# Turning softmax probabilities by 32x32 blocks and transfers, not by TensorE

## What is computed

```
# layer 0                              # layer 1 (8 heads of 64)
h = x @ W                              q, k, v = h @ Wq.T + bq, h @ Wk.T + bk, h @ Wv.T + bv
e = leaky_relu(h@a0 + (h@a1).T)        scores = q @ k.T / 8, -inf where adj == 0
alpha = softmax(e, -1e9 where adj==0)  attn = softmax(scores)
out = concat([alpha @ h, h])           out = (attn @ v) @ Wo.T + bo
x1 = layernorm(x + out)                y = layernorm(x1 + out)
```

## Time and profile before

| | us |
|---|---|
| median of 3 runs (lowest to highest) | 3468.7 (3466.77 to 3469.16) |
| the profiled execution, its whole time | 3468.5 |
| its span in the trace | 3466.6 |
| busy: TensorE, VectorE, ScalarE, GpSimd | 3412.3, 2688.1, 2510.2, 1616.8 |
| one steady round | 106.0 |

### The profile page before, as it was taken

The page is one execution under the profiler, slowest core; times in us unless marked ns, Lnnn a source line. Parts: engine busy times, 40 slices in busy tenths (PEclk is TensorE's granted clock), DMA queues, the critical chain, the costliest instruction groups (busy, mean ns, idle before and its releaser), DMA issues.

```text
span 3466.6 us, 65791 instructions
## 1 busy us (share of the span) xinstructions
PE 3412.3 (98%) x23168; PEld 2903.8 (84%) x23168; DVE 2688.1 (78%) x7607; ACT 2510.2 (72%) x5382; POOL 1616.8 (47%) x1542
## 2 busy tenths in 40 slices
PE   6999999999999999999999999999999999999998
PEld 5888888888888888888888888888888888888886
DVE  5787777877777877778777778777787777877776
ACT  4776777776777767777777777677777777777775
POOL 2544454445454444544454544445444454444443
PEclk8999999999999999999999999999999999999999
DMA  3000011000111010110001110001100011100100
GB/s 128 19 22 28 25 38 38 31 26 22 34 38 38 20 31 25 37 38 31 26 21 36 38 35 22 26 31 38 38 25 32 19 38 37 32 25 25 31 13 25
DMA packets 59652, 111.19 MB, mean 32 GB/s; under 512 B 6720, under 2 KB 7488, under 8 KB 59328
## 3 DMA queue, kind: packets, MB, share of 16 engines
q1 hardware_dynamic: 59328, 106.99, 9.6%
HBM read 73.41 MB, written 33.55 MB: 31 GB/s over the span
## 4 chain that ended last, share of the span: by engine, by line
PE 97%; DVE 1%; ACT 1%; issue 0%; DMA 0%; POOL 0%; SPq 0%; ACTq 0%; DVEq 0%; POOLq 0%
PE R_bank L541 47%; PE O_bank L629 14%; PE T_bank L613 14%; PE S_bank L603 13%; PE L_bank L541 5%; PE L_bank L532 3%; PE L_bank L556 0%; DMA prob<-WkT 0%; POOL turned L985 0%; DVE prob L900 0%; PE O_bank L541 0%; DMA alpha<-a 0%; ACT tokens L674 0%; DVE n_wide L946 0%; ACT prob L734 0%
## 5 line engine op out<-in xcount | busy, mean ns | idle before, releaser
L965 POOL TENSOR_TENSOR prob<-prob,rsum 128x512 f32<-128x512 f32 x1024 | 1059.5, 1041 | 1309.3 <-DVE rsum L906 1307.4
L734 ACT ACTIVATE prob<-prob,negmax 128x512 f32<-128x512 f32 x1024 | 739.6, 722 | 323.3 <-DVE negmax L900 314.9
L659 ACT ACTIVATE probT<-T_bank 128x512 fp32r<-128x512 f32 x1024 | 579.0, 594 | 220.8 <-PE T_bank L613 214.6
L900 DVE CUSTOM_DVE_ANT_0 prob<-S_bank,mask 128x512 f32<-128x512 f32 x1024 | 695.5, 679 | 2.2 <-PE S_bank L603 1.1
L794 DVE TENSOR_TENSOR probT<-T_bank,probT 128x512 fp32r<-128x512 f32 x1024 | 675.9, 683 | 5.1 <-ACT probT L659 3.1
L613 PE MATMUL T_bank<-ident,prob 128*128 128x128 f32 x4096 | 597.7, 276 | 3.1 <-DVE probT L794 3.1
L629 PE MATMUL O_bank<-probT,v_st 128*128 128x256 f32 x4096 | 586.6, 288 | 2.8 <-DVE probT L794 2.8
L906 DVE RECIPROCAL rsum<-psum_row 128x1 f32<-128x1 f32 x1024 | 164.9, 161 | 542.7 <-PE S_bank L603 303.4
L613 PEld LDWEIGHTS T_bank<-ident,prob 128*128 128x128 f32 x4096 | 459.0, 141 | 106.1 <-issue 93.8
L629 PEld LDWEIGHTS O_bank<-probT,v_st 128*128 128x128 f32 x4096 | 522.2, 190 | 21.5 <-issue 11.5
L603 PE MATMUL S_bank<-qk_pair 64*128 64x512 f32 x3072 | 494.1, 426 | 2.5 <-DVE negmax L900 2.2
(11 more groups left out here) (84 smaller groups left out, 4374.0 us busy)
## 6 DMA issues: line engine op xcount, KB each, us to landing
tokens<-xT SPq DMA_DIRECT2D x128, 256.0 KB, 3.0
tokens<-x SPq DMA_DIRECT2D x128, 256.0 KB, 2.7
out<-tokens SPq DMA_DIRECT2D x128, 256.0 KB, 2.1
tokens<-adj SPq DMA_DIRECT2D x1, 1024.0 KB, 6.5
tokens<-WqT SPq DMA_DIRECT2D x1, 1024.0 KB, 5.5
prob<-WkT SPq DMA_DIRECT2D x1, 1024.0 KB, 7.9
tokens<-WvT SPq DMA_DIRECT2D x1, 1024.0 KB, 6.5
prob<-WoT SPq DMA_DIRECT2D x1, 1024.0 KB, 5.0
```

The source lines that it names most:

```text
L659: act.activation(dst, src, ACT.Copy).then_inc(done, 1)
L734: act.activation(prob[:, slot, :], prob[:, slot, :], ACT.Exp, bias=negmax[:, slot:slot + 1], scale=-1.0, accum_out=psum_row[:, slot:slot + ...
L900: dve.tensor_tensor_reduce(prob[:, slot, :], S_bank[s % 2][:, :], mask[:, s % 8 // 2, :], -SCALE, HUGE, ALU.add, ALU.min, negmax[:, slot:s ...
L965: pool.tensor_tensor(prob[:, slot, :], prob[:, slot, :], rsum[:, slot:slot + 1].to_broadcast([P, N]), ALU.mult).then_inc(p_norm, 1)
```

## The change

Its main part is the way of a probability tile from `exp` to `weigh`. `turn` and both `T_bank`s are gone from TensorE. Tiles are kept in `prob` interleaved by 32 columns, four tiles to a buffer `ph` (a pair of heads by a half of the queries), three buffers. After the normalisation, VectorE turns the sixteen 32x32 blocks of a tile in place (`vt`). SyncE then moves blocks between the four groups of 32 partitions: for every buffer 4 steps `mv`, each of 4 transfers of 32 partitions by 4 runs of 512 bytes (64 KB). They land in `turned_lo_prob` (two buffers). `hi` on ScalarE copies from there into `turned_hi_prob` (one buffer), and `lo` on GpSimd subtracts in place. `weigh` reads both.

Around it: one tile in four is normalised by ScalarE (`norm`), three by GpSimd (`pnorm`, L998); `O_bank` becomes two banks, `L_bank` too; `qk_pair`, `turned` and `alpha` have one buffer for two; the copy of `N` on VectorE (`n_wide`) is gone, ScalarE reads the bank; all five plans are written anew.

```diff
-            def turn_probs(R, s):
-                pe.wait_ge(p_norm, R.n(32, s + 1))
-                if due(R.n(16, s // 2)):
-                    pe.wait_ge(t_lo[s % 2], R.n(16, s // 2))
-                for c in range(T):
-                    last = pe.transpose(T_bank[s % 2][:, c * P:(c + 1) * P], prob[:, s % SLOTS, c * P:(c + 1) * P],
-                                        ident[:, :])
-                last.then_inc(t_mm, 1)
             def weigh(R, g):
-                pe.wait_ge(t_lo[w], R.n(16, 4 * pair + 2 * half + 2))
+                pe.wait_ge(p_lo, R.n(32, 4 * ph + 4))
-                if w == 0 and due(R.n(16, g)):
-                    pe.wait_ge(o_sum, R.n(16, g))
+                if w == 0 and due(R.n(16, g - 2)):
+                    pe.wait_ge(o_sum, R.n(16, g - 2))
+            def turn_blocks(R, s):
+                if s % 4 == 3:
+                    if due(R.n(16, s // 2 - 3)):
+                        dve.wait_ge(pv_mm, R.n(16, s // 2 - 3))
+                    dve.wait_ge(p_normed_act, R.n(8, s // 4 + 1))
+                else:
+                    dve.wait_ge(p_normed_pool, R.n(24, 3 * (s // 4) + s % 4 + 1))
+                dve.transpose(prob_tile(R, s), prob_tile(R, s)).then_inc(p_turned, 1)
+            def move_probs(R, m):
+                ph, a = m // 4, m % 4
+                if a == 0:
+                    sp.wait_ge(p_turned, R.n(32, 4 * ph + 4))
+                own = slice(BLK * a, BLK * (a + 1))
+                for d in range(4):
+                    sp.dma_start(turned_lo_prob[BLK * d:BLK * (d + 1), ph % 2, a, :, :].bitcast(F32),
+                                 prob[own, prob_buffer(R, ph), d::4, :, :].rearrange("p c j i -> p c (j i)")).then_inc(p_moved[prob_buffer(R, ph)][a], 16)
+            def probs_hi(R, m):
+                ph, a = m // 4, m % 4
+                if a == 0 and due(R.n(16, 2 * ph)):
+                    act.wait_ge(pv_mm, R.n(16, 2 * ph))
+                act.wait_ge(p_moved[prob_buffer(R, ph)][a], moved_count(R, ph))
+                split_hi(turned_hi_prob[:, a, :, :], turned_lo_prob[:, ph % 2, a, :, :].bitcast(F32), p_hi)
+            def normalise_last(R, p):
+                act.wait_ge(p_inv, R.n(32, s + 1))
+                act.activation(prob_tile(R, s), prob_tile(R, s), ACT.Copy,
+                               scale=rsum[:, slot_of(R, s):slot_of(R, s) + 1]).then_inc(p_normed_act, 1)
+            def probs_lo(R, m):
+                pool.wait_ge(p_hi, R.n(32, m + 1))
+                pool.tensor_tensor(turned_lo_prob[:, ph % 2, a, :, :], turned_lo_prob[:, ph % 2, a, :, :].bitcast(F32),
+                                   turned_hi_prob[:, a, :, :].bitcast(F32), ALU.subtract).then_inc(p_lo, 1)
...
-    "weigh scores turn turn",
+    "scores k1 N",
```

510 lines of the change are left out of this document (260 added, 250 removed).

## The result

The changed kernel takes 3642.9 us (median of 4 runs, 3632.3 to 3644.6) against 3468.9 for the kernel before, measured beside it: a ratio of 1.0495, 95% interval 1.0474 to 1.0516. It is 5% slower, where 3078 us and 11% faster had been forecast. The profiled execution has a span of 3640.5 us and a mean clock of 0.948.

What follows compares the result with a forecast made beforehand. TensorE, busy 98%, was taken as the bound: 3466.6 less 485 us of turns gives a 2982 us floor, plus 78 of waits and 16 at the ends, 3076 us of span, so 3078 us, 11% faster; range 3000 to 3160.

Steps and rivals of the forecast that it cites:

- The step that failed is SyncE's: SyncE's queue: 4096 transfers join 384, each taken at 0.5 us to issue, so a round's issues fit under 90.8 us.
- the rival of the moves: SyncE's queue or the DMA engines set the pace above 0.785 us a transfer; 3526 us at 0.80; chance 0.09.
- It hides if the queue keeps up: Last block turn to last `hi` takes 10.1 us, hidden because a buffer needs 11.3 us of a 90.8 us round.
- The clock at 1.00: TensorE's granted clock stays at 1.00; its falling through new gaps was part of a no-gain rival, 3470 us, chance 0.03.
- The 78 us of waits at the one high buffer: TensorE waits for GpSimd's `lo` at the single `turned_hi_prob`: 2.5 us a round over 31 rounds, 78 us.
- TensorE's own saving: Removing the probability turns takes 485 us off TensorE, other matmuls staying the same in number and shape; floor 2982 us.
- VectorE's block turn: On VectorE, 1024 block turns at 0.60 us replace 1024 `lo`, a free exchange leaving VectorE at 2688 us.
- the landing: A transfer to SBUF lands some 2.1 us after SyncE issues it.
- the DMA engines hide: The moves' 524,288 runs of 512 bytes at 0.045 us take 1475 us on each DMA engine, half the floor, hidden.
- The rivals of slow turns: Block turns on VectorE take 1.0 us, VectorE reaches 3098 us at 100%, 3190 us with waits; chance 0.07.
- a normalisation at 1.27 us: GpSimd's slower normalisation, or late `hi`, makes GpSimd and the one high buffer the bound: 3200 to 3340 us; chance 0.15.
- the lock between GpSimd and block turns: VectorE's block turns and GpSimd exclude each other, adding 19 us a round to GpSimd: 3370 us; chance 0.06.

Runs made afterwards that it cites:

- third_landing: The changed kernel with three landing buffers instead of two, the low half of Wo left out for room: 3646.6 us.
- quarter_moves: The changed kernel with one of four transfers of every step, the rest of the landing buffer keeping zeros: 3314.1 us.
- quarter_moves_sum_first: quarter_moves with VectorE's `sum` moved ahead of the leaky ReLU and mask of a tile: 3249.2 us.
- quarter_runs: The changed kernel with all 4096 transfers, each moving only one of its four runs of 512 bytes: 3569.3 us.
- three_quarter_moves: The changed kernel with three of four transfers of every step, a quarter of the landing buffer keeping zeros: 3320.7 us.
- through_dram: The changed kernel with each buffer going to DRAM in four stores and back in four loads, 8 transfers instead of 16: 3595.4 us.
- spread_queue: split_queue_sum_first with each of ScalarE's four issues for a buffer between two other steps: 3236.4 us, ratio 0.9325 to the kernel before.
- split_queue: The changed kernel, complete, with the fourth transfer of every step issued by ScalarE, four in a row for a buffer: 3420.8 us.
- split_queue_sum_first: split_queue with VectorE's `sum` moved ahead of the leaky ReLU and mask of a tile: 3350.2 us.
- projections_late: The changed kernel with only the two V projections made later in TensorE's order: 3780.6 us.
- long_runs: The changed kernel with the same bytes in runs of 2 KB, `x1T` in permuted order and the V projections later on TensorE: 3746.9 us.

## Why the prediction was wrong, step by step

**The step that failed is SyncE's.** It took 0.5 us a transfer from bursts of four loads from DRAM, 70 us a round, 77 at the dearer burst; the runs show a median of 601 ns and some 0.65 us from start to start, nearly whatever the bytes, 90 to 92 us a round. The single row of 0.80 was above the truth, the bursts below it; the transfers from SBUF to SBUF had no row.

**The threshold failed more than the price.** For the rival of the moves I wrote that one transfer must cost over 0.785 us. By that rule 0.646 would have been harmless. It compared the queue's work with a whole round, as if SyncE could issue at any time. But it can issue only when block turns are done, and these stand in VectorE's order behind the output projection. With the 21.4 us a round that it stands, the threshold for a round as long as before is (106.0 - 21.4) / 140 = 0.604 us (0.62 with the 19.4 us of the round shown); that is an estimate, since the stand is the changed kernel's. The mechanism of that rival (chance 0.09) is the one that came true: it gave 3526 us, 3643 were measured.

**"It hides if the queue keeps up"** was the condition on which three `prob` and two landing buffers rested. It didn't keep up: `hi` waited 377 us for transfers. The two landing buffers were enough (third_landing); whether the three `prob` were, no run shows.

**The clock at 1.00** was argued from one window with 2.9 us idle in 60. Some 3 us in one piece, ahead of the output projection, are another thing: the clock was 0.50 in the next 6 us. Over the execution it was 0.948, and 5.2% of TensorE's 3170 busy us are 165 us, as an estimate of what it cost; with the queue relieved (quarter_moves) it was still 0.968.

**The 78 us of waits at the one high buffer** were looked for in the wrong place. Where the queue isn't full, TensorE waits 49 us for `lo`, less than that, but 98 us for `oT`, which no step of mine mentions. I summed the work between pairs of weighted sums, and not the work between the last one and the output projection, which the change cut from 5.1 to 0.9 us. And I saw in the earlier trace rows that the leaky ReLU on `alpha` can be stretched beside GpSimd, gave GpSimd 1000 us more to do, and put the consequence at nothing: once a round it came out at 3.8 us, ahead of the `sum` for which the output projection waits. Taking out turns alone already returned 78% of their price, and no more. The 171 us between quarter_moves_sum_first and the forecast are TensorE's remaining waits (203 us in it, 45 in the kernel before, 94 expected) and the clock at 0.985, as far as is known; how they divide was not tried.

**Right were** TensorE's own saving in number and shape; VectorE's block turn (0.60 forecast, three in 1.88 us measured, 685 ns long); ScalarE's normalisation (0.70 forecast, 717 ns) and `hi` (630, 625); GpSimd's `lo` (1.27, 1292 ns long) and its total (2661, 2656); and the landing (2.1, 2.0). None of them is what set the time. That the DMA engines hide was right, their 1475 us for the moves were not: all traffic of the queue takes 0.378 x 3640.5 = 1376 us, and from the three quarters of the runs that quarter_runs leaves out (0.167 x 3567.5 = 596 us) a run of 512 bytes takes 0.032 us, not 0.045, so some 1040 us for all. The rivals of slow turns and of a normalisation at 1.27 us (1.06 measured) are out with these numbers. So is the lock between GpSimd and block turns: these take 660 / 688 / 712 ns (minimum, median, maximum) beside a GpSimd that is 73% busy. For the operations of VectorE with two inputs in SBUF the same view shows the other case, here the mask over `alpha`, which took 685 to 687 ns before:

```profile
L881 DVE CUSTOM_DVE_ANT_0 alpha<-alpha,mask x128: 685/687/1812, 39.6 to 3447.0; 128x512 f32<-128x512 f32 x128
```

Both agree with the Trainium skill, "SBUF — State Buffer", section "Who interferes with whom": one SBUF input does not contend, two do. For the mask this costs 43 us of VectorE in the changed kernel (mean 1020 ns, 686 before). The leaky ReLU, the same kind of operation, is the dearer one where the queue is relieved: 3841 ns at most in quarter_moves, 1530 before. So the lock was a rival for the wrong instruction.

**The excess by size.** 322 us are the full queue (changed kernel against three_quarter_moves), 65 the order of one sum, with the leaky ReLU beside GpSimd and the clock behind, 171 the rest: 558 of the 565 us between forecast and result.

## What to carry to other kernels

Count the instructions of every queue, not only its bytes, at the price of the same kind of transfer, and set their sum against the time in which the queue has something to issue, not against the whole round. When the orders of the steps are written anew, list the work that lies between the two ends of every chain through other engines, before and after: a chain that has lost its cover costs its gap, and clock behind it. When work is put on GpSimd, look for VectorE's operations with two inputs in SBUF that will run beside it, and for what waits behind them. A second issuing queue is cheap on an engine that computes only if each issue has an operation to run beside.

## What the runs showed of the hardware

- An issue of a 64 KB transfer from SBUF to SBUF by SyncE takes 585 ns at least, 601 in the median, and 0.644 us from start to start in a full queue; with a quarter of the runs, or with runs four times as long, 591. A load of `x` from DRAM took 328 ns in the median in the kernel before, 334 in quarter_moves, and 588 in the changed kernel, where it stands right behind moves. In through_dram the loads back took 430, the stores 648.
- On ScalarE's queue the same transfer takes 593 ns (spread_queue) to 625 (split_queue) in the median, a lone load 335. With each issue between two operations ScalarE stood 6 us for issue in all; in groups of four (split_queue_sum_first) 294 us.
- Runs of 512 bytes and of 2 KB from SBUF to SBUF took the DMA engines about the same time for the same bytes: 36.1% of 3779 us (projections_late) and 37.2% of 3745 (long_runs).
- Behind one gap of some 3 us on TensorE (3.13 of 6 us busy) the granted clock was 0.50 in the next 6 us, in which TensorE was busy for 5.66.
- A block turn of 128x512 float32 takes 685 ns on VectorE, and 712 at most beside a GpSimd that was busy 73% of the time. Operations with two SBUF inputs were stretched: the mask from 687 to 1812 ns, the leaky ReLU from 681 to 3841, beside four GpSimd operations in a row.
